# Key sums of all four groups in the scores' buffer, two buffers of keys by token, and both halves of the feed-forward's input product in one piece

## The reference

```
x = x + 0.5 * ffn(layernorm(x))
x = x + attn(layernorm(x))
x = x + 0.5 * ffn(layernorm(x))

ffn(x):  s = x @ Win + bin_                      # 512 -> 64
         h = relu(s[..., None] * W1 + b1)        # 16 hidden values for each of the 64
         g = sum(h * W2) + b2
         return g @ Wout + bout                  # 64 -> 512

attn(x): q, k, v = split(x @ w_attn)             # 16 heads of 32
         q, k = elu(q) + 1, elu(k) + 1
         S += k outer v;  z += k                 # running over the tokens of a batch
         y = (q @ S) / (sum(q * z) + 1e-6)
         return y @ w_proj
```

## Time and profile before

| | |
|---|---|
| median of 3 runs | 2386.6 us (2385.26 to 2386.83) |
| span of the profiled execution | 2384.9 us |
| TensorE matmuls, busy | 2291.9 us, 96% |
| VectorE busy | 1936.4 us, 81% |
| ScalarE busy | 1423.0 us, 60% |
| GpSimd busy | 812.4 us, 34% |
| DMA, mean | 47 GB/s |

### The profile page before, as it was taken

The page is one execution under the profiler, slowest core; times in us unless marked ns, Lnnn a source line. Parts: engine busy times, 40 slices in busy tenths (PEclk is TensorE's granted clock), DMA queues, the critical chain, the costliest instruction groups (busy, mean ns, idle before and its releaser), DMA issues.

```text
span 2384.9 us, 74819 instructions
## 1 busy us (share of the span) xinstructions
PE 2291.9 (96%) x32578; PEld 1761.2 (74%) x32578; DVE 1936.4 (81%) x3346; ACT 1423.0 (60%) x2267; POOL 812.4 (34%) x864
## 2 busy tenths in 40 slices
PE   3999999999999999999999999999999999999995
PEld 2777777777777777777777777777777777777774
DVE  6679888888888889888888888888888888887766
ACT  5556566556566556556556557556656556656554
POOL 5223333333333333333333233333233333233222
PEclk7899999999999999999999999999999999999998
DMA  5001111111111111111111101111101111101111
GB/s 173 20 13 45 38 38 56 55 48 45 38 38 55 55 54 39 40 36 56 55 55 37 55 21 56 55 55 37 56 20 56 55 55 37 56 20 38 37 38 37
DMA packets 49657, 111.53 MB, mean 47 GB/s; under 512 B 8241, under 2 KB 10289, under 8 KB 45234
## 3 DMA queue, kind: packets, MB, share of 16 engines
q1 hardware_dynamic: 49330, 106.74, 15.3%
HBM read 72.12 MB, written 34.60 MB: 45 GB/s over the span
## 4 chain that ended last, share of the span: by engine, by line
PE 73%; DVE 16%; issue 5%; POOL 4%; ACT 1%; SPq 1%; DMA 0%; DVEq 0%; POOLq 0%; ACTq 0%
PE bank L1014 33%; PE att L1014 13%; PE att L1043 5%; PE att L1130 5%; PE att L1155 5%; DVE st L681 3%; DVE res L735 3%; DVE acc_psum L719 2%; PE att L1146 2%; PE bank L1118 2%; PE bank L1081 2%; POOL z L370 2%; PE att L1072 2%; DVE yl L698 1%; PE bank L1166 1%
## 5 line engine op out<-in xcount | busy, mean ns | idle before, releaser
L461 ACT ACTIVATE xhat<-res,nmr,rstd 128x512 f32<-128x512 f32 x384 | 302.2, 808 | 354.8 <-DVE nmr L689 292.0
L478 ACT ACTIVATE ffr<-ffs,b1c,w1c 128x512 f32<-128x512 f32 (+2 forms) x544 | 424.4, 805 | 20.0 <-DVE acc_psum L719 13.9
L719 DVE SCALAR_TENSOR_TENSOR acc_psum<-ffr,w2c,acc_psum 128x512 f32<-128x512 f32 (+2 forms) x510 | 379.0, 743 | 48.7 <-ACT ffr L478 27.8
L374 POOL TENSOR_SCALAR_AFFINE_SELECT A<-A 128x512 f32<-128x512 f32 x256 | 157.2, 638 | 704.5 <-ACT A L438 704.5
L362 POOL TENSOR_TENSOR res<-res,hbout 128x512 f32<-128x512 f32 x256 | 352.1, 1393 | 4.0 <-ACT xhat L461 3.4
L681 DVE BATCH_NORM_STATS2 st<-res 128x6 f32<-128x512 f32 x384 | 260.9, 679 | 17.6 <-DMA res<-in_L_attn_x_dram 11.8
L370 POOL TENSOR_TENSOR z<-qT,z 128x512 f32<-128x512 f32 x128 | 165.8, 1295 | 269.8 <-DVE zc L765 119.6
L1014 PE MATMUL att<-xh,wa_h 128*128 128x512 f32 x584 | 235.7, 404 | 1.9 <-DVE xl L698 1.9
L1014 PE MATMUL att<-xl,wa_h 128*128 128x512 f32 x584 | 231.8, 397 | 0.0
L1014 PE MATMUL att<-xh,wa_l 128*128 128x512 f32 x584 | 231.7, 397 | 0.0
L1014 PE MATMUL bank<-wa_h,xh 128*128 128x512 f32 x504 | 214.6, 426 | 0.0
(11 more groups left out here) (142 smaller groups left out, 4969.0 us busy)
## 6 DMA issues: line engine op xcount, KB each, us to landing
xf<-scratch SPq DMA_DIRECT2D x128, 256.0 KB, 4.5
res<-in_L_attn_x_dram SPq DMA_DIRECT2D x31, 1024.0 KB, 5.4
out_dram<-res SPq DMA_DIRECT2D x31, 1024.0 KB, 4.8
scratch<-rden SPq DMA_DIRECT2D x128, 8.0 KB, 1.6
res<-in_L_attn_x_dram SPq DMA_DIRECT2D x4, 256.0 KB, 3.4
kT<-in_L_attn_w_attn_dram SPq DMA_DIRECT2D x1, 1024.0 KB, 5.5
qT<-in_L_attn_w_attn_dram SPq DMA_DIRECT2D x1, 1024.0 KB, 11.9
v<-in_L_attn_w_attn_dram SPq DMA_DIRECT2D x1, 1024.0 KB, 16.3
```

The lines of the kernel that those rows point to most:

```text
L374: eng.affine_select(out=A[:, h, :, :], in_=A[:, h, :, :], compare_op=ALU.is_ge, fill=0.0, base=0, pattern=[[0, 4], [1, P]], channel_multip ...
L461: eng.activation(xhat[t % 2][:, :], res[b % SLOTS][:, t, :], ACT.Identity, bias=nmr[:, n, b % 2, t:t + 1], scale=rstd[:, n, b % 2, t:t + 1 ...
L478: eng.activation(ffr[i % 2][p, w], ffs[p, w], ACT.Relu, bias=b1c[p, i:i + 1], scale=w1c[p, i:i + 1]).then_inc(s_hr, 1)
L719: eng.scalar_tensor_tensor(psum[p, w], r[p, w], w2c[p, i:i + 1], psum[p, w], ALU.mult, ALU.add).then_inc(s_hm, 1)
```

## The change

The buffer `z2` goes. The key sums of all four groups are written into the memory of `A` (as `z`, a view of four rows of 512), so a scan waits for no `den` of its own block; it waits for the attention of the block before (`s_num`) and, once, for the last reader of `w_proj` (`s_walo`). `ktok` becomes two buffers, used in turn, and its copy waits for the last update but one. What `z2` held at the start (`Wout`, `bout`) is now loaded into the two `ktok`. In TensorE's list `ff_in(j, 1)` moves up behind `ff_in(j, 0)`, ahead of `values(j, 1, 0)`.

```
-        ktok = sb("ktok", [P, C])
+        ktok = [sb(f"ktok{i}", [P, C]) for i in range(2)]
...
-        z2 = sb("z2", [P, 2, BLK])
...
+        z = wp_st
+        wo_st, bout_st = ktok[0], ktok[1]
...
             def key(b, t):
                 e.wait_ge(s_kt, nth_update(b, t))
 
-                e.wait_ge(s_up, nth_update(b, t) - 1)
-                copy(ktok[:, :], bank[spot["key", b, t][0]][:, :], s_ktok)
+                e.wait_ge(s_up, nth_update(b, t) - 2)
+                e.wait_ge(s_wol, 1)
+                copy(ktok[nth_update(b, t) % 2][:, :], bank[spot["key", b, t][0]][:, :], s_ktok)
...
                 e.wait_ge(s_elu[1], 4 * b + g + 1)
 
-                e.wait_ge(s_den, 4 * b + g - 1)
-                e.wait_ge(s_mbout, 1)
-                e.wait_ge(s_wol, 1)
+                e.wait_ge(s_num, 4 * b)
+                e.wait_ge(s_walo, 4)
                 if not first:
                     e.wait_ge(s_zc, carried(b - 1, g))
-                eng.tensor_tensor_scan(z2[:, g % 2, :], kT[:, g, :], kT[:, g, :], 0.0 if first else zc[:, g:g + 1],
+                eng.tensor_tensor_scan(z[:, g, :], kT[:, g, :], kT[:, g, :], 0.0 if first else zc[:, g:g + 1],
                                        ALU.add, ALU.bypass).then_inc(s_scan, 1)
...
                 if on(j - 1) or on(j + 2):
                     ff_in(j, 0)
+                    ff_in(j, 1)
                 if on(j):
                     values(j, 1, 0)
-                if on(j - 1) or on(j + 2):
-                    ff_in(j, 1)
-                if on(j):
                     values(j, 1, 1)
                     scores(j, 0)
```

More of the change, by code:

```diff
@@ L221, in macaron_kernel @@
         for j in range(NB + 2):
-            give(ATT + RING, ("k", j, 0), ("k", j, 1), ("q", j, 0), ("q", j, 1), ("k", j, 2), ("k", j, 3), ("q", j, 2),
-                 ("den", j, 0), ("q", j, 3), ("v", j, 0), ("key", j, 0))
+            give(ATT + RING, ("k", j, 0), ("k", j, 1), ("q", j, 0), ("q", j, 1), ("k", j, 2), ("k", j, 3), ("q", j, 2), ("den", j, 0), ("q", j, 3), ("v", j, 0), ("key", j, 0))
             if on(j - 1) or on(j + 2):
@@ L234, in macaron_kernel @@
             give(RING, ("y", j, 2))
-            give(ATT + RING, ("xT", j + 1, 2), ("xT", j + 1, 3), ("y", j, 3), ("o0", j - 1, 0), ("o1", j + 2, 0),
-                 ("key", j, 3), ("up", j, 3), ("o0", j - 1, 1), ("o1", j + 2, 1), ("o0", j - 1, 2), ("o1", j + 2, 2),
-                 ("o0", j - 1, 3), ("o1", j + 2, 3))
+            give(ATT + RING, ("xT", j + 1, 2), ("xT", j + 1, 3), ("y", j, 3), ("o0", j - 1, 0), ("o1", j + 2, 0), ("key", j, 3), ("up", j, 3), ("o0", j - 1, 1), ("o1", j + 2, 1), ("o0", j - 1, 2), ("o1", j + 2, 2), ("o0", j - 1, 3), ("o1", j + 2, 3))
         wa_st = [qT, kT, v]
         wp_st = A[:, :, :, :].rearrange("p h g n -> p h (g n)")
+        z = wp_st
+        wo_st, bout_st = ktok[0], ktok[1]
         WALO = {1: 1, 0: 2, 2: 3}
@@ L277, in _ @@
             load(1)
-            eng.dma_start(z2[0:1, 1, :], bout.rearrange("(a n) -> a n", a=1)).then_inc(s_bout, 16)
+            eng.dma_start(bout_st[0:1, :], bout.rearrange("(a n) -> a n", a=1)).then_inc(s_bout, 16)
             for h in range(4):
@@ L290, in _ @@
             for h in range(2):
-                eng.dma_start(z2[M * h:M * h + M, 0, :], Wout).then_inc(s_wo, 16)
+                eng.dma_start(wo_st[M * h:M * h + M, :], Wout).then_inc(s_wo, 16)
             for n in (0, 2):
@@ L354, in wout_lo @@
                 e.wait_ge(s_woh, 1)
-                eng.tensor_tensor(wo_l[:, :], z2[:, 0, :], f32(wo_h[:, :]), ALU.subtract).then_inc(s_wol, 1)
+                eng.tensor_tensor(wo_l[:, :], wo_st[:, :], f32(wo_h[:, :]), ALU.subtract).then_inc(s_wol, 1)
             def bias(half, b, t):
@@ L364, in zsum @@
             def zsum(b, g):
-                z = z2[:, g % 2, :]
                 e.wait_ge(s_scan, 4 * b + g + 1)
@@ L369, in zsum @@
                     e.wait_ge(s_zc, carried(b, g))
-                eng.tensor_tensor(z, qT[:, g, :], z, ALU.mult).then_inc(s_zq, 1)
+                eng.tensor_tensor(z[:, g, :], qT[:, g, :], z[:, g, :], ALU.mult).then_inc(s_zq, 1)
             def mask(b, t, h):
@@ L547, in _ @@
             e.wait_ge(s_wo, 32)
-            copy(wo_h[:, :], z2[:, 0, :], s_woh)
+            copy(wo_h[:, :], wo_st[:, :], s_woh)
             e.wait_ge(s_wa[0], 16)
@@ L764, in carry @@
                 e.wait_ge(s_scan, 4 * b + g + 1)
-                eng.tensor_copy(zc[:, g:g + 1], z2[:, g % 2, BLK - 1:BLK]).then_inc(s_zc, 1)
+                eng.tensor_copy(zc[:, g:g + 1], z[:, g, BLK - 1:BLK]).then_inc(s_zc, 1)
             def rec(b):
@@ L1097, in den @@
                 for t in range(TILES):
-                    op = eng.matmul(o[D * t:D * t + D, 0:P], heads_of[:, g, :], z2[:, g % 2, t * P:t * P + P],
+                    op = eng.matmul(o[D * t:D * t + D, 0:P], heads_of[:, g, :], z[:, g, t * P:t * P + P],
                                     start=g == 0, stop=g == 3)
@@ L1165, in update @@
                         d, n = slice(D * h, D * h + D), slice(g * P + D * h, g * P + D * h + D)
-                        op = eng.matmul(o[d, g * D:g * D + D], ktok[:, n], v[:, t, n], start=True, stop=True)
+                        op = eng.matmul(o[d, g * D:g * D + D], ktok[nth_update(b, t) % 2][:, n], v[:, t, n], start=True, stop=True)
                 op.then_inc(s_up, 1)
@@ L1181, in _ @@
             o = take("bout", 0, 0)
-            eng.matmul(o[:, :], tri[0:1, :], z2[0:1, 1, :], start=True, stop=True).then_inc(s_mbout, 1)
+            eng.matmul(o[:, :], tri[0:1, :], bout_st[0:1, :], start=True, stop=True).then_inc(s_mbout, 1)
             for n in range(2):
```

## The result

The changed kernel takes 2411.05 us (2410.96 to 2411.09, 4 runs) against 2386.72 us of the kernel before on the same chip: a ratio of 1.010, 95% interval 1.0088 to 1.0112. It is slower by 24.3 us. The profiled execution has a span of 2409.2 us, 24.3 above the 2384.9 of before.

What follows compares the result with a forecast made beforehand. TensorE's own list was taken as the bound. From the 2384.9 us span, 6.1 for a saved break and 0.8 for one stop came off, 36.0 for stops was added: 2414.0, stated as 2415 us, range 2407 to 2426 (chance 0.78).

Steps and rivals of the forecast that it cites:

- The bound: Whole kernel: TensorE's own list, its matmuls and the steps between them, sets the time; matmuls in its pipe 96% of the span.
- The waits that I called hidden: Scans and buffers: old and new semaphore waits costed at nothing; the scans' freed wait could bring at most 2.5 us.
- Term 1: Joined values on TensorE: one change of shape less in each of 32 iterations, 6.1 us off.
- Term 2: Joined ff_in: TensorE runs out of instructions and stops 1.24 us in each of 29 iterations, 36.0 us added.
- bound of 2.4 for a free landing: ff_in before: an instruction packet landing up to 2.4 us after its start costs nothing; with the change, up to 0.90.
- The sum: Whole run: 2384.9 - 6.1 - 0.8 + 36.0 = 2414.0 us of span, given as a median of 2415.
- Rival 1: Joined ff_in: instruction store deeper than two packets or packets asked for earlier, so no stops; 2379.7 us, chance 0.07.
- rival 3: ff_in: packets late more often or a second one late, 0.3 to 0.6 us more an iteration; 2424 to 2433, chance 0.07.
- Rival 2: Even iterations: the stop is paid back as waits for GpSimd's product and rec go, 13.8 us; 2401, chance 0.08.
- Rival 4: Even iterations: the scans' freed wait lets VectorE and GpSimd be early, the POOL wait goes, 6.4 us less; no chance given.

Runs made afterwards that it cites:

- 2: The changed kernel with ff_in in two parts again, values(j, 1, 0) between them, key sums in A and two ktok kept: 2385.60 us.
- Experiment 5: The changed kernel with ff_in in two parts again and the four den in one piece behind values(j, 0, 1): 2362.29 us.
- experiment 3: The changed kernel with three matmuls of values put between the two parts of ff_in: 2397.40 us.
- experiment 1: The kernel before with only the two parts of ff_in joined, buffers as they were: 2411.84 us.
- experiment 4: The changed kernel with 48 small matmuls and their loads added once at TensorE's start: 2426.28 us.

## Why the prediction was right, and where it was off

**The bound.** TensorE's own list set the time before and sets it after. The waits that I called hidden stayed hidden: 2 shows no difference, within 0.1%, for all the buffers' edits together, and the scans no longer wait on TensorE at all.

**Term 1**, 6.1 us for one break less. Seen as 2.99 against 2 x 1.60 on the chain in the same place, and as 5.7 us in 29 iterations. Right for `values`; iterations 0, 30 and 31 gained 0.35 each and not 0.2, so the term was 0.6 too small. Experiment 5 shows that the size does not carry over: a break between full matmuls and `den` costs more, since the `den` too take longer in short pieces (0.28 us more for two of 16 than for one of 32).

**Term 2**, 36.0 us in 29 stops. Measured 36.1 from start to start, 33.1 as idle time alone. That it fits so closely is luck: two inputs were off by 0.2 us each, and the errors cancel. The packets landed 2.37 us after the start of `ff_in` on the mean (2.03 to 2.72), where I had carried over 2.17 from the kernel before; and a landing was free up to about 1.12 (2.37 less the mean loss of 1.24), where I had 0.90. My bound of 2.4 for a free landing in the kernel before was too strict: iteration 6 landed at 2.53 there and lost nothing, though 11 and 22, at 2.51 and 2.48, lost 0.1. The 12 us of experiment 3 were worked out from the same two inputs. The place was forecast as pairs 157 and 99; it is 168 and 88 at first, 155 and 101 at the end, since an iteration holds a little more than eight packets' instructions. In the even iterations it is one or two pairs further on than in the odd ones beside them. Experiments 1, 3 and 4 bear the mechanism out: it comes with the order alone, its size goes with the time between two edges, and its place goes with the count of instructions before it. What stays a reading of the trace and is not shown by itself: that two packets are held, and the 3 us split into asking, transfer and use. The Trainium skill's figure of 2048 instructions held for TensorE ("Runtime: NRT & Kernel Launch", section on instruction fetch mechanics) does not agree with these traces, in which TensorE stops after 222 pairs from the start and 128 pairs after a stop. The two lines of 16 KiB that the same section of the Trainium skill names are in keeping with them (the 257 packets of the page are 4.21 MB, 16.4 KB each), though no run here counts the lines by itself.

**The sum** was 4 us too high, 2415 against 2411; against the profiled span it is 4.8, 2414.0 against 2409.2. The largest part is the start, which the sum left out: 2.6 of the 3.0 us by which the first scores came sooner. I had put the stop there at nothing, though its packet is on no fixed place: in the profiles of this study its idle time is between 0.8 and 3.0 us, and there is none in experiment 4, where `ff_in` also began 6 us later. And the sum had no term for the clock, whose return to the full level 4.4 us sooner gave 1.45 of the 2.6. Another 1.3 us are between the scores and the next `ff_in`, where 2.1 us went and I had counted 0.8; 0.6 are term 1; 0.3 are behind the start of the last `ff_in`. No run shows the quicker start as a gain of the change: the first scores come at 103.0 in experiment 1, with the new order, and at 101.8 in 2, with the old one.

**The rivals.** Rival 1 (a deep store) and rival 3 (more stops an iteration) did not come true. Experiment 4 shows that the third was not far off: with 48 pairs more ahead, four iterations have two stops, and the single ones are longer (1.4 us on the mean against 1.1). Rival 2 (paid back by the waits of even iterations) fell: both waits stand as before, 0.41 us for GpSimd's product and 0.46 ahead of `ff_in`. Rival 4 did not happen either: the wait for GpSimd stood at 0.41, and only the reordering of 5 made it go.

## What to carry to other kernels

Where an engine runs very short instructions, count them: about 127 matmuls with their loads came per packet here, and a stretch that was through them in less than some 3.3 us stopped without any wait that a semaphore shows ("issue" amid equal instructions). The 3.3 is an estimate: 2.02 us of cover and 1.24 of loss in the changed kernel, 2.87 and 0.41 in experiment 3, both 3.3. So the six full matmuls between two bursts were a packet's cover and joining the bursts had to be priced with it. An edit that only lifts a constraint is worth nothing until the order uses it: the buffers gave 0 us as they were, and 36 us with the `den` put together in a bank that nobody waits for (2349.73 us, the best kernel of this study).

## What the runs showed of the hardware that was not expected

The place of TensorE's stops for instructions is set by the count of everything before them: 96 instructions more at the start moved a stop by 48 pairs some 370 us later, and again in the last `ff_in` at 2402, and the run took 15 us longer (2426.28 against 2411.05). In that run TensorE was granted half the clock for 3.4 us just behind a stop of 1.74 us, which cost 1.5 us; none of the other stops in the 29 full iterations of that run and of the changed kernel was followed by this, and that the stop brought it about is not shown. The `den` (128 rows by 32 columns, 128 wide) cost 1.01 us as one piece of 32 and 1.29 as two of 16.
